# Summing vector messages unreduced: the Tanh layer's message path rewritten and spread over one more pipeline step

## The reference, cut to what matters

```
h     = sqrt(2) * relu(emb @ W1 / sqrt(10))                    # 16 hidden values of an edge
w     = (h @ W2 / 4).reshape(E, 7, 16, 8)                      # wa_s, wb_s, wa_g, wb_g, wc, wd, we
xs,xv = 16 scalars and 16 vectors: 8 of the source node and 8 of the target node
s_out = PW_S * (xs.wa_s + (xv.y1).wb_s / sqrt(3))              # 8 scalars
g_out = the same with wa_g, wb_g                               # 8 gates
v_out = PW_V * (y1 (xs.wc) + xv.wd + (xv y2 W3J121).we, ...)   # 8 vectors of 3
msg   = [1.593 tanh(s_out), 1.593 tanh(g_out) * v_out] * norm  # 8 + 24 numbers
out   = segment_sum(msg, edge_dst)
```

## Time and profile before

| | us |
|---|---|
| median of 3 runs | 14662.81 (14660.83 to 14662.97) |
| the profiled execution | 14665.89 |
| its span | 14664.2 |
| mean granted TensorE clock | 0.885 |

### The profile page before, as it was taken

The page is one execution under the profiler, slowest core; times in us unless marked ns, Lnnn a source line. Parts: engine busy times, 40 slices in busy tenths (PEclk is TensorE's granted clock), DMA queues, the critical chain, the costliest instruction groups (busy, mean ns, idle before and its releaser), DMA issues. The chain is left out here.

```text
span 14664.2 us, 437528 instructions
## 1 busy us (share of the span) xinstructions
PE 12078.2 (82%) x114342; PEld 9157.5 (62%) x114342; DVE 12076.0 (82%) x30182; ACT 7889.6 (54%) x23572; POOL 9995.6 (68%) x10550
## 2 busy tenths in 40 slices
PE   1555555555566999999999999988899999999999
PEld 1444444445455666666666666666677777777777
DVE  5777777777768999999999999986677777777776
ACT  0455555555544666666666666647544444444443
POOL 4777777777765666666666666637677777777775
PEclk8666666666668999999999999989899999999999
DMA  3555555555542222222222222218511111111111
GB/s 95 83 87 87 86 87 87 86 87 87 87 73 41 36 36 36 36 36 36 36 36 36 36 36 36 36 20 282 174 25 25 25 25 25 25 25 25 25 25 24
DMA packets 2705893, 840.24 MB, mean 57 GB/s; under 512 B 2232498, under 2 KB 2650073, under 8 KB 2704124
## 3 DMA queue, kind: packets, MB, share of 16 engines
q1 hardware_dynamic: 2212179, 616.76, 21.2%
q0 software_dynamic: 312320, 178.52, 9.3%
q10 hardware_dynamic: 181250, 43.25, 1.4%
HBM read 610.22 MB, written 226.58 MB: 57 GB/s over the span
## 5 line engine op out<-in xcount | busy, mean ns | idle before, releaser
L1401 POOL DMA_INDIRECT w_rows<-table,w_idx x9375 | 8949.5, 955 | 3848.0 <-issue 2539.0
L1384 PE MATMUL w_p_deg<-w_hot_lo,w_hot_row 128*128 128x196 bf16 x6250 | 1802.8, 336 | 1570.3 <-DVE w_hot_lo L1329 1512.1
L1637 PE MATMUL w_p_w<-w_w,w_ht 128*128 128x256 f32 x12500 | 3033.1, 390 | 0.0
L1637 PEld LDWEIGHTS w_p_w<-w_w,w_ht 128*128 128x128 f32 x12500 | 2272.7, 190 | 404.3 <-issue 0.2
L1869 DVE TENSOR_TENSOR w_prod<-w_p_xe,w_he 128x512 f32<-128x512 f32 x3125 | 2137.6, 684 | 4.1 <-PE w_p_xe L2012 4.1
L1619 ACT ACTIVATE w_ht<-w_p_h 128x512 f32<-128x512 f32 x1875 | 851.0, 526 | 2270.5 <-PE w_p_h L1651 2270.5
L1358 ACT CAST w_counts<-w_p_count 128x784 uint8<-128x784 f32 x1875 | 1247.7, 706 | 1451.8 <-PE w_p_count L1385 1442.0
L1384 PEld LDWEIGHTS w_p_deg<-w_hot_lo,w_hot_row 128*128 128x128 bf16 x6250 | 832.6, 133 | 1698.2 <-issue 1604.8
L1385 PE MATMUL w_p_count<-w_hot_lo,w_hot_row 128*128 128x196 bf16 x6250 | 1813.8, 337 | 0.0
L1147 ACT ACTIVATE w_dist<-row_iota,w_negrel 128x32 f32<-128x32 f32 x6250 | 1453.3, 309 | 301.0 <-issue 273.8
L2035 PE MATMUL w_p_sgt<-w_prod,w_wc 128*32 128x128 f32 x25000 | 1331.9, 284 | 85.4 <-ACT w_sgt L1948 64.1
(11 more groups left out here) (220 smaller groups left out, 20437.7 us busy)
## 6 DMA issues: line engine op xcount, KB each, us to landing
counts<-w_counts SPq DMA_DIRECT2D x1250, 122.5 KB
d_small<-counts SPq DMA_DIRECT2D x388, 392.0 KB
w_rows<-table,w_idx POOLq DMA_INDIRECT x9375
w_rel_row<-rel_row SPq DMA_DIRECT2D x625, 120.0 KB
w_edge<-e SPq DMA_DIRECT2D x625, 80.0 KB
w_idx<-src SPq DMA_DIRECT2D x1875, 2.5 KB
w_negrel<-negrel SPq DMA_DIRECT2D x1875, 2.5 KB
w_nodes<-split SPq DMA_DIRECT2D x1875, 2.0 KB
```

Source lines behind the costliest of these rows:

```text
L1384: nc.tensor.matmul(p_deg[:], hot_row[s2][:, b, :], hot_lo[s2][:, b, :], start=False, stop=False, skip_group_check=True)
L1401: pool.indirect_dma_start(out=rows[:, t, :], out_offset=None, in_=table[0:N, :], in_offset=bass.IndirectOffsetOnAxis(ap=idx[:, t:t + 1], a ...
L1637: last = nc.tensor.matmul(p_w[(g.base * len(BANKS) + bank) % WBANKS][:, (t - t0) * 256:(t - t0 + 1) * 256], ht[g.slot(UNROLL)][:, k, t * P ...
```

## The change

Layer 1's messages are no longer reduced before they are summed over the window. Where `msg` held 64 gated target weights, 8 scalars and 24 reduced vector numbers, `mix` holds for each edge and each of the 8 outputs 44 numbers: 8 gated source weights, then 8 gated target weights, the scalar, and 3 times 9 unreduced products. The last 36 of each are summed over the window.

- `sum_window` is replaced by `QuarterSums`, the class that layer 3 uses: `sum_edges` gives each of four 32-row quarters of PSUM one tile (four matmuls of 288 columns) and the fifth tile in four pieces of 72 columns; VectorE folds the products nine to one (`fold`, a copy and a reduce); `sum_quarters` adds the quarters with one matmul.
- `vector_weights` moves from at(3), in four pieces, to at(4), in one; the gating multiplies `p_wv` with the gate in one instruction for source and target half (`gated_weights`), and the three vector products read `mix` in SBUF in place of `p_wv` in PSUM. The message work runs at(4), at(5) and at(6), and DEPTH is 6.
- ScalarE no longer copies target weights; it copies the along part of `p_out` instead, makes `hot` a step later, and copies `sgt` before it casts `xt`. Target rows are copied before source rows.
- GpSimd's gathers no longer wait for VectorE's products; `dots` comes one step earlier and waits for the fourth product of the group two steps ahead of it. The later stage for the target vectors handles 72 columns and has 8 small copies more in place of as many others.

The diff, cut to its core (the class `QuarterSums` is in the kernel before, L1171 ff.):

```diff
-DEPTH = 5
+DEPTH = 6
@@ window_pass_1, GpSimd
-                    for t in range(T):
-                        wait_count(pool, prod_ready, g.times(T, t - 3 * T))
-                        pool.nop(nofuse=True)
-                        gather_tile(pool, a["table"][1], idx[s], rows[s], t, gathered[s])
+                    gather_rows(pool, a["table"][1], idx[s], rows[s], gathered[s])
+                if g := at(1):
...
+                    wait_count(pool, prod_ready, g.times(T, 4 - 2 * T))
+                    nc.gpsimd.tensor_mul(dots[s2][:], v16[s][:], spread(unit[s][:], [P, T, MUL1, 3], 2)).then_inc(dots_ready, 1)
@@ VectorE
+            def gated_weights(g):
...
+                vec.tensor_mul(gated[:], along[s2][:], gate[s2][:, :, 8:16]).then_inc(gated_ready, 1)
+                done(dve, wv_ready, g)
+                free(dve, w.mix_ready, g, 2)
+                vec.tensor_mul(mix[s2][:, :, :, 0:ENDS], p_ends, spread(gate[s2][:, :, 8:16], [P, T, 8, ENDS], 3)).then_inc(wv_used, 1)
+            def vector_products(g, k0, k1):
...
+                for k in range(k0, k1):
+                    vec.tensor_mul(to[:, :, :, 17 + 9 * k:25 + 9 * k], to[:, :, :, 0:8], spread(v16[s][:, :, 0:8, k], [P, T, 8, 8], 2))
+            def fold(g):
...
+                vec.tensor_copy(held[:, 0:72].rearrange("p (w c) -> p w c", c=9), p_mix[:, :, 0:9])
+                vec.tensor_reduce(held[:, 72:MSG1].rearrange("p (w k) -> p w k", k=3), p_mix[:, :, 9:OWN].rearrange("p w (k u) -> p w k u", u=9),
+                                  AX.X, ALU.add).then_inc(w.held_ready, 1)
             def step(at):
+                if g := at(5):
+                    gated_weights(g)
                 if g := at(1):
                     wg.one_hot(dve, g)
                 if g := at(3):
                     tile_products(g, 0)
+                if g := at(5):
+                    vector_products(g, 0, 1)
+                if g := at(6):
+                    w.add_window(dve, g)
...
                 if g := at(3):
                     tile_products(g, 1)
+                if g := at(5):
+                    vector_products(g, 1, 3)
+                    along_products(g)
...
                     tile_products(g, 3)
+                if g := at(5):
+                    fold(g)
                 if g := at(3):
                     tile_products(g, 4)
-                    vector_products(g)
@@ TensorE
                     expand(g, 0)
+                if g := at(6):
+                    w.sum_quarters(pe, g)
                 if g := at(4):
                     contract(g, 4)
...
-                    free(pe, gate_ready, g, 3)
-                    free(pe, vout_ready, g, 3)
+                    free(pe, w.acc_added, g, 5)
                     free(pe, dst_copied, g, 1)
                     wg.product(pe, g)
...
                     expand(g, 3)
-                    vector_weights(g, 1, 2)
+                if g := at(4):
+                    vector_weights(g)
+                if g := at(5):
+                    done(pe, msg_ready, g)
+                    done(pe, gate_copied, g)
+                    w.sum_edges(pe, g, lambda t: tile(g, t), lambda q: quarter(g, q))
+                if g := at(3):
                     contract(g, 2)
-                    vector_weights(g, 2, 3)
                     expand(g, 4)
-                    vector_weights(g, 3, T)
                     contract(g, 3)
...
-                    w.sum_window(pe, g, msg[g.slot(2)], msg_ready)
```

More of the change, by code:

```diff
@@ L57 @@
 SPLIT = 3
-SUM1, MSG1 = 64, 96
+MSG1 = 96
 EPS = 1e-5
@@ L1739, in window_pass_1 @@
         prod = [sb(f"prod{s}", [P, 4, P]) for s in range(2)]
-        prodv = sb("prodv", [P, T, 24 * 9])
-        wdst = [sb(f"wdst{s}", [P, T, 64]) for s in range(2)]
-        redv = sb("redv", [P, T, 24])
         sgt = [sb(f"sgt{s}", [P, GE]) for s in range(2)]
         bent = [sb(f"bent{s}", [P, T, G_ROWS]) for s in range(2)]
+        along = [sb(f"along{s}", [P, T, 8]) for s in range(2)]
+        gated = sb("gated", [P, T, 8])
         stack = sb("stack", [P, WIDE])
         gate = [sb(f"gate{s}", [P, T, 16]) for s in range(2)]
-        msg = [sb(f"msg{s}", [P, T, MSG1]) for s in range(2)]
+        mix = [sb(f"mix{s}", [P, T, 8, SLOT]) for s in range(2)]
         w2_in = sb("w2_in", [HID1, 7, MUL1, OUT1])
@@ L1870, in tile_products, with gates @@
                                spread(he[g.slot(UNROLL)][:, t * P:(t + 1) * P], [P, 4, P], 1)).then_inc(prod_ready, 1)
[L1872 to L1878, removed]
+            def gates(g):
+                s2 = g.slot(2)
+                done(dve, bent_ready, g)
+                free(dve, gate_copied, g, 2)
+                vec.scalar_tensor_tensor(gate[s2][:], bent[s2][:], TANH_GAIN, spread(weight[g.slot(UNROLL)][:], [P, T, 16], 2),
+                                         ALU.mult, ALU.mult).then_inc(gate_ready, 1)
@@ L2014, in expand, with vector_weights, tile, quarter @@
                 last.then_inc(xe_ready, 1)
-            def vector_weights(g, t0, t1):
-                if t0 == 0:
-                    free(pe, wv_used, g, 1)
-                    free(pe, wdst_ready, g, 1)
-                for t in range(t0, t1):
-                    last = nc.tensor.matmul(p_wv[:, t * P:(t + 1) * P], he[g.slot(UNROLL)][:, t * P:(t + 1) * P], wv[:], start=True, stop=True)
-                if t1 == T:
-                    last.then_inc(wv_ready, 1)
+            def vector_weights(g):
+                done(pe, bent_ready, g)
+                done(pe, along_ready, g)
+                free(pe, wv_used, g, 1)
+                for t in range(T):
+                    last = nc.tensor.matmul(p_wv[:, t * P:(t + 1) * P], he[g.slot(UNROLL)][:, t * P:(t + 1) * P], wv[:], start=True, stop=True)
+                last.then_inc(wv_ready, 1)
+            def tile(g, t):
+                return mix[g.slot(2)][:, t, :, 8:SLOT]
+            def quarter(g, q):
+                return slice(2 * OWN * q, 2 * OWN * (q + 1)), mix[g.slot(2)][:, 4, 2 * q:2 * q + 2, 8:SLOT]
             def contract(g, t):
@@ L2046, in step @@
                     expand(g, 0)
+                if g := at(6):
+                    pe.wait_ge(dst_copied, g.times(1, 5) if at(2) else G)
+                    w.sum_quarters(pe, g)
                 if g := at(4):
@@ L2052, in step @@
                     done(pe, sgt_last, g)
-                    pe.wait_ge(dst_copied, g.times(1, 3) if at(2) else G)
-                    free(pe, w.acc_added, g, 1)
+                    free(pe, wv_used, g, 1)
                     for t in range(T):
@@ L2061, in step @@
                     expand(g, 2)
-                    vector_weights(g, 0, 1)
                 if g := at(1):
@@ L2091, in step @@
                     last.then_inc(xt_mm, 1)
-                if g := at(4):
-                    done(pe, gate_copied, g)
-                    pe.wait_ge(dst_copied, g.times(1, 4) if at(1) else G)
-                    w.sum_window(pe, g, msg[g.slot(2)], msg_ready)
             pipeline(pe, step)
```

139 lines of the change are left out of this document (63 added, 76 removed).

## The result

The changed kernel takes 14778.28 us (median of 4 runs, 14773.08 to 14780.48) against 14661.82 before (4 runs, 14658.87 to 14662.97): ratio 1.008, 95% interval 1.0067 to 1.0092. It is 116 us slower; 14787 and slower were forecast.

The account below looks back on a forecast made before the run. TensorE's queue was taken to bound layer 1: 8.30 - 0.42 + 0.07 - 0.06 + 0.70 = 8.59 us per step against 8.40, +119 us, plus 5 for draining: 14787 us. The 8-in-10 range was 14635 to 14950.

Parts of the forecast that it names:

- item 1: TensorE's vector_weights: 1.78 us in four pieces become 1.26 together, contract(3) behind expand(4) costs 0.10 more: -0.42 us per step.
- 2. contract(3) to expand(0): TensorE's way to expand(0) through ScalarE's copy and cast: 1.69 us for 1.62, about 1.0 idle: +0.07 per step.
- 3. expand(0) to contract(4): TensorE: the 0.18 wait for the copy goes, sum_quarters comes between; 0.51 us for 0.57: -0.06 per step.
- 4. sum_edges: New TensorE work in the middle of the step, scaled by columns from layer 3: +0.70 us per step.
- the 0.10 that the prediction counted as waits for the gate: TensorE's mean wait per step for VectorE's gate ahead of wg.product, 0.10 us, expected to go.
- its signs of being wrong: No idle ahead of expand(0), TensorE waiting for products, VectorE's rows longer beside gathers, or granted clock below 1.00.
- So 8.30 is TensorE's own queue: Layer 1 before: TensorE's queue takes 8.30 us per step and sets the pace; VectorE's gate adds 0.10.
- Rival A: VectorE, not TensorE, sets layer 1's pace: step of 7.5 us, -560 us, 14100; chance 0.11.
- The 7.5 us that the prediction gave VectorE: VectorE's busy time per changed step: at most 8.29 us, rather 7.5.
- Rival B: Gathers hold VectorE's products that read SBUF twice: 9.9 us per step, +940 us, 15600; chance 0.05.
- Rival C: No change: sum_edges and sum_quarters at lower bounds 0.57 and 0.13, step 8.31 to 8.45, about 14655; chance 0.14.

Follow-up runs that it names:

- experiment 2: Changed kernel with p_xt issued ahead of contract(2) and the cast of xt ahead of the copy of sgt: 14663.0 us.
- experiment 4: Changed kernel with twelve more matmuls that no one reads behind p_xt: 14743.5 us.
- experiment 1: Changed kernel with ScalarE's cast of xt ahead of its copy of sgt: 14798.9 us.
- experiment 7: Kernel before with p_out in the second bank of p_wv, wg.product freed from the gate, vector_weights left in four places: 14456.0 us, ratio 0.9853.
- experiment 5: Kernel before with the five matmuls of vector_weights together behind expand(3) instead of in four places: 14737.7 us.
- experiment 8: Kernel before with VectorE's reduce cut to a third of its columns: 14657.5 us, ratio 0.999.

## Why the prediction was right, and where it was not

The sign, the size and the mechanism of the loss held: the changed step is TensorE's queue with an open wait for the cast of xt in it. By its items:

1. vector_weights together: 8000.41 to 8001.68 = 1.27, forecast 1.26; expand(4) to contract(3) 0.33, as forecast.
2. contract(3) to expand(0): 8002.97 to 8004.69 = 1.72, forecast 1.69, with 0.88 idle, forecast about 1.0. Experiments 2 and 4 show that this is a wait on the critical path; experiment 1 that the copy's place has no part in it.
3. expand(0) to contract(4): 0.47, forecast 0.51.
4. sum_edges: 8001.68 to 8002.31 = 0.63, forecast 0.70. It is the second piece, 0.13 against 0.23, that was mis-sized: contract(2) starts sooner behind it than the follower in layer 3.

These make a steady step of 8.50 rather than 8.59. The mean is 8.59 all the same, through two terms that the sum left out. The program has its steps written out four at a time in a loop, and the one at the loop's turn is longer, about 8.68: some 0.04 in the mean (before, such steps took 8.69 for 8.30, and this is the 0.10 that the prediction counted as waits for the gate). And the 22 steps of fallen clock cost some 1.4 us each, 0.05 in the mean. The prediction named that opening only among its signs of being wrong; it was real, and worth 35 us (experiment 4). So the point of 14787 is 9 us off partly by luck.

The step that failed is the reading of the kernel before: "So 8.30 is TensorE's own queue". It was not. With the wait for the gate taken out, the same queue returns after 8.07 (experiment 7). How much of that is TensorE's own stays open, since VectorE is idle for only 0.1 us of such a step. The rest was the way from p_out over tanh and gate to wg.product, and 0.22 of it stood in an ordinary step, inside the 0.50 that item 1 put down to the first piece of the weights. No idle time is marked there in the earlier trace rows, since the modelled end of the matmul before covers it; the earlier trace rows show only what sticks out, 0.10 in the mean. The sum came out because the change frees wg.product from the gate as well as joining the weights, so the whole 0.50 did go; that 0.22 of it went by another cause is luck. The price shows in experiment 5, whose expectation rested on that reading and missed by 270 us.

Rival A (VectorE sets the pace) is refuted by experiment 8, and the weight loads' share of 70% was no measure of TensorE's room in this stretch: the step hung on TensorE's queue and a wait in it. The 7.5 us that the prediction gave VectorE in the changed step was too low as well: it is 4937.41/625 = 7.90, since gated takes 0.54 in the mean (below) and the other new instructions about as much as was taken away. That cost nothing in a step of 8.59.

Rival B (gathers beside products that read SBUF twice) expected VectorE to be held by the gathers. It is held mainly in one place, the small product gated, and there by the dots; its products of mix and v take 0.59 in the mean, as before. It is the gathers that are longer. In the changed kernel, VectorE's and GpSimd's timelines:

```profile
8003.69 0.49 DVE L1884 TENSOR_TENSOR w_gated<-w_along,w_gate 128x40 f32<-128x40 f32 x1
...
8007.24 1.10 DVE L1893 TENSOR_TENSOR w_mix<-w_mix,w_v 128x320 f32<-128x320 f32 x2
8008.27 0.36 DVE L1898 TENSOR_TENSOR w_mix<-w_gated,w_unit 128x120 f32<-128x120 f32 x1
```

```profile
8003.48 0.64 POOL L1825 TENSOR_TENSOR w_dots<-w_v,w_unit 128x240 f32<-128x240 f32 x1 [1.07 <-DMA w_negrel<-negrel]
...
8007.45 2.14 POOL L1401 DMA_INDIRECT w_rows<-table,w_idx  x1 [0.30 <-issue]
```

gated takes 0.49 where it meets the dots, and 0.19 where it does not (8304.18 us); the gather beside three products takes 2.14 for 0.94. The Trainium skill ("SBUF — State Buffer", Who interferes with whom) says that a VectorE instruction with two SBUF inputs contends with a GpSimd instruction that reads SBUF, and not with one that only writes it. The row of gated agrees. The prediction took from it that the gathers would hold no product, which came true; that the products could hold the gathers it did not ask. That they do is read from where the rows lie, and was not tried by itself: over the changed stretch, gathers that lie beside none of the products of L1893 and L1898 take 0.96 us in the mean, and those that lie some 1.2 us or more beside them 2.1. Two SBUF inputs alone don't explain it: in the kernel before, gathers beside the subtraction of the earlier trace rows take 0.94 to 0.98, no longer than others. What sets the products apart stays open. In the changed kernel the long gathers cost nothing that the lists show, since GpSimd still waits for DMAs in a step of 8.59. In experiment 2, where GpSimd sets the pace, a gather takes 1.22 in the mean for 0.95 before; five of them make 1.35 us more per step, a share of what that experiment lost that no run took away by itself.

Rival C (the new pieces at their lower bounds, 0.57 and 0.13) did not come: sum_edges at 0.63 and sum_quarters at 0.23 lie between its sizes and the forecast's 0.70 and 0.28, and the step of 8.50 lies above its 8.31 to 8.45.

Left open: why the clock falls in just these 22 steps, where the gap ahead of expand(0) is the same 0.88 in the others; and where the one run of 14790 in experiment 2 comes from.

## What to carry to other kernels

Where instructions are moved out of the shadow of a wait, their time is not saved: the wait stays, and they cost their length at the new place. Before a moved piece is priced, ask whether its measured start-to-start time holds a wait that the trace does not mark, by looking at what the next instruction waits for, and whether it always starts the same time behind the end of that. And try the parts of a large change one by one: here one of its small edits, another bank for p_out, is worth 216 us by itself in the kernel before, and the change as a whole, which has it too, is 116 us slower.

## What the runs showed of the hardware

A gap of 0.88 us per step of 8.5 us in an otherwise busy TensorE was followed, in 22 of 623 steps, by some 3 us at a granted clock of 0.50; with some 0.7 us of the gap filled by unread matmuls it was 1.00 throughout and the kernel 35 us faster. Gathers, which took 0.94 to 0.99 us in the kernel before, took up to 2.17 in the changed one, the longest beside VectorE's products of L1893 and L1898; that these are the cause is read from the rows alone. A product of 40 elements with both inputs in SBUF took 0.19 us alone and 0.49 beside GpSimd's dots.
